# An attention loop on TensorE: scores, weighing and projection ahead of the subtraction of maxima and the turned scores

## The reference

```python
h = _L0_tok_ref(x, ...)                       # pairs of rows through a matrix, plus their mean, layer norm
h = h + _L0_attn_ref(_layernorm(h), ...)
h = h + _L0_ffn_ref(_layernorm(h), ...)       # shared FFN and 16 experts of 752 tokens each
...
latent_kv = (k + v) @ W_down_kv               # k = x @ W_k, v = x @ W_v
scores = einsum('bhqd,bhkd->bhqk', qh, k_rec) / sqrt(d) * exp(-0.01 * abs(t - t'))
out = einsum('bhqk,bhkd->bhqd', softmax(scores), v_rec) ; out @ W_o
```

## Time and profile before

| | before |
|---|---|
| time, median of 3 runs | 1873.16 us (1870.95 to 1875.5) |
| time of the profiled execution | 1870.4 us |
| its span | 1868.6 us |
| TensorE busy | 1689.0 us, 90% of the span |
| VectorE busy | 1224.8 us, 66% |
| ScalarE, GpSimd busy | 902.6 us, 950.2 us |
| mean granted clock of TensorE | 0.956 of 2.4 GHz |

### The profile page before, as it was taken

The page is one execution under the profiler, slowest core; times in us unless marked ns, Lnnn a source line. Parts: engine busy times, 40 slices in busy tenths (PEclk is TensorE's granted clock), DMA queues, the critical chain, the costliest instruction groups (busy, mean ns, idle before and its releaser), DMA issues.

```text
span 1868.6 us, 46715 instructions
## 1 busy us (share of the span) xinstructions
PE 1689.0 (90%) x15566; PEld 1232.2 (66%) x15566; DVE 1224.8 (66%) x3739; ACT 902.6 (48%) x1965; POOL 950.2 (51%) x945
## 2 busy tenths in 40 slices
PE   6874899999999999579999669999999999999997
PEld 5873566666666665357777537777777777777775
DVE  3883788888888888384778655555555555555551
ACT  4442566666666665244233634444444444444442
POOL 3771244444444443272224054666666666666665
PEclk9995999999999999789999779999999999999999
DMA  5522455555555555242010232333333334333322
GB/s 189 176 94 50 106 121 126 134 123 133 132 127 128 129 136 116 50 133 51 26 34 26 96 123 86 102 101 97 93 93 100 98 100 101 101 101 99 101 34 28
DMA packets 220234, 186.52 MB, mean 100 GB/s; under 512 B 165625, under 2 KB 200953, under 8 KB 214009
## 3 DMA queue, kind: packets, MB, share of 16 engines
q1 hardware_dynamic: 193272, 141.11, 28.2%
q0 software_dynamic: 26880, 44.36, 11.5%
HBM read 134.49 MB, written 50.44 MB: 99 GB/s over the span
## 4 chain that ended last, share of the span: by engine, by line
PE 70%; DVE 12%; issue 8%; POOL 4%; SPq 2%; ACT 2%; DMA 2%; DVEq 1%; POOLq 0%; ACTq 0%
PE psum L1678 26%; PE psum L1695 13%; PE psum L1542 6%; PE psum L1560 4%; DVE arena L1086 4%; DVE psum L1094 3%; PE psum L1441 3%; PE psum L1498 2%; PE psum L1395 2%; PE psum L1409 2%; PE psum L1463 2%; PE psum L1420 2%; POOL hidden L570 2%; POOL arena L575 1%; PE psum L1508 1%
## 5 line engine op out<-in xcount | busy, mean ns | idle before, releaser
L1678 PE MATMUL psum<-arena,hidden 128*128 128x376 f16 x3072 | 493.1, 323 | 0.9 <-DVE arena L1320 0.9
L634 POOL TENSOR_TENSOR arena<-arena 128x376 f16<-128x376 f32 x320 | 317.4, 994 | 343.9 <-ACT arena L727 342.5
L1678 PEld LDWEIGHTS psum<-arena,hidden 128*128 128x128 f16 x3072 | 301.0, 98 | 188.9 <-issue 1.6
L727 ACT ACTIVATE arena<-arena 128x376 f16<-128x376 f32 (+5 forms) x610 | 287.3, 474 | 54.0 <-DVE arena L1250 43.1
L1086 DVE CUSTOM_DVE_ANT_0 arena<-psum,constants 128x188 f32<-128x188 f32 x768 | 228.0, 345 | 106.8 <-PE psum L1395 105.4
L727 ACT ACTIVATE arena<-psum 128x188 f32<-128x188 f32 (+7 forms) x457 | 168.1, 398 | 257.6 <-PE psum L1658 74.9
L926 ACT ACTIVATE arena<-psum 128x376 f32<-128x376 f32 x256 | 123.7, 483 | 342.2 <-PE psum L1678 342.2
L1330 DVE SCALAR_TENSOR_TENSOR arena<-psum,arena 128x376 f32<-128x376 f32 x256 | 140.8, 550 | 189.3 <-ACT arena L926 187.8
L1695 PE MATMUL psum<-hidden,arena 128*128 128x256 f16 (+1 forms) x2304 | 256.6, 273 | 0.0
L1695 PEld LDWEIGHTS psum<-hidden,arena 128*128 128x128 f16 (+1 forms) x2304 | 229.8, 103 | 21.8
L776 ACT ACTIVATE arena<-psum 128x564 f32<-128x564 f32 x256 | 164.0, 641 | 98.6 <-PE psum L1409 97.0
(11 more groups left out here) (156 smaller groups left out, 2644.2 us busy)
## 6 DMA issues: line engine op xcount, KB each, us to landing
arena<-q_halves SPq DMA_DIRECT2D x384, 47.0 KB, 2.4
arena<-k_halves SPq DMA_DIRECT2D x384, 47.0 KB, 2.3
arena<-e_g SPq DMA_DIRECT2D x16, 1024.0 KB, 5.1
arena<-e_u SPq DMA_DIRECT2D x16, 1024.0 KB, 5.2
arena<-e_d SPq DMA_DIRECT2D x16, 1024.0 KB
arena<-x_t SPq DMA_DIRECT2D x32, 376.0 KB, 3.5
weighed<-arena POOLq DMA_DIRECT2D x32, 376.0 KB, 3.9
q_halves<-arena SPq DMA_DIRECT2D x32, 188.0 KB, 3.1
```

The costliest lines, as they stand in the source:

```text
L634: nc.gpsimd.tensor_tensor(dst, f, hi, ALU.subtract).then_inc(ready, 1)
L727: return nc.scalar.activation(dst, src, ACT.Copy, scale=scale)
L1678: last = mm(bank[2 * (s % 2) + i][:, 0:CHUNK], w_, a, start=n == 0, stop=n == 5)
```

## The change

In each step of the attention loop TensorE issues S, W, J, T, U where it issued S, T, U, W, J. The parts themselves, their waits, and the orders of the other engines are as before.

```diff
@@ -1515,10 +1515,10 @@
             def batch(b, par):
                 for j in range(HP):
                     scores(b, par, j)
+                    weigh(b, par, j)
+                    job(b, par, j)
                     take_max(b, par, j)
                     turned_scores(b, par, j)
-                    weigh(b, par, j)
-                    job(b, par, j)
 
             batches(pe, batch)
             meet(pe)
```

## The result

| | before | after |
|---|---|---|
| time, median | 1874.33 us (1870.95 to 1879.8, 4 runs) | 1978.4 us (1974.67 to 1979.41, 4 runs) |
| time of the profiled execution | 1870.4 us | 1974.67 us |
| VectorE busy share of 400 to 500 us | 87% | 76% |
| mean granted clock | 0.956 | 0.959 |

The changed kernel takes 1.0553 times as long (95% interval 1.0533 to 1.0574). The forecast was 1968, the range 1918 to 1992.

A forecast was written before the change was run, and what follows sets the result against it. TensorE and VectorE were taken to wait for each other in turn, 18.04 us a batch. New waits of 5.17 us less 1.85 won, over 27 batches, plus about 5 at the ends, gave 1873 + 95 = 1968 us; range 1918 to 1992.

The forecast's parts named there:

- Wait 1: TensorE's J4 waits for VectorE's add_out, which comes behind D3 and so U3; loss 1.48 us a batch.
- Wait 2: TensorE's J2 waits for ScalarE's copy of XF, behind E1 and so T1; loss 0.75 us a batch.
- Wait 3: TensorE's W7 waits for the turned maxima, VectorE's low_max behind D6; loss 1.01 us a batch.
- Wait 4: TensorE's S7 waits for VectorE's R6, reckoned from U5 by way of D5; loss 0.59 us a batch.
- Wait 5: TensorE's W1, W3, W5 wait for ScalarE's E of the step before; loss 0.28 us each, 0.84 a batch.
- Wait 6: TensorE's J1 waits for VectorE's normalized rows, made behind D0; loss 0.50 us, between 0.19 and 0.81.
- the gain: Six TensorE waits ahead of T4, T5, T7, W7, S0 and T0 go: up to 1.85 us a batch.
- the ends: The five batches at each end have only parts of the waits and gain: together about 5 us.
- A: Releasers of W and J come earlier too, so the new waits are not there: 1819 us; chance 0.07.
- B: Only VectorE's releases bind, ScalarE answers faster: 1.7 us a batch, +51, 1924 us; chance 0.12.
- D: Gain and loss cancel within about 0.2%, or the engine does not do what is written: 1873 us; chance 0.02.
- C: TensorE's clock falls to 0.50 once in each of 27 batches, near 2.9 us each: 2046 us; chance 0.05.

The follow-up runs named there:

- decay_last: Changed kernel with VectorE's small work (except inverse sums and moments' aggregation) ahead of D in each step and ScalarE's XF copy ahead of E1: 1934.61 us, ratio 1.0335.
- xf_early: Changed kernel with ScalarE's copy of XF ahead of E in its step 1 instead of behind it: 1965.97 us, ratio 1.0469.
- divisors_first: step5_only with SP's four reads of the inverse sums ahead of its write of the query halves: 1910.11 us, ratio 1.0185.
- inverse_in_4: divisors_first with VectorE's aggregation of the row moments in step 7 and its inverse sums in step 4: 1924.39 us, ratio 1.0258.
- weigh_late: J alone moved ahead (S, J, T, U, W in a step), with J5 also waiting for ScalarE's copy (os_ready): 1932.84 us, ratio 1.0309.
- step5_only: Kernel before with J ahead of T and U in step 5 alone, J5 also waiting on os_ready: 1867.47 us, ratio 0.9965.

## Why the prediction was right

The mechanism was the one that was put down, and each wait was where it was said. Below is what each cost in the batch shown: how long behind its forerunner a group starts, less how long that is where nothing holds it. Beside it stands the price in the prediction.

- Wait 1, J4 on add_out: 418.95 - 417.21 - 0.26 = 1.48; foretold 1.48. D3 starts 0.52 behind U3 where 0.60 was taken, and J4 0.12 behind add_out where 0.05 was taken; the two cancel, so that the match to 0.01 is luck.
- Wait 2, J2 on XF: 413.31 - 412.15 - 0.31 = 0.85; foretold 0.75.
- Wait 3, W7 on low_max: 405.49 - 404.06 - 0.41 = 1.02; foretold 1.01.
- Wait 4, S7 on R6: S7 loads 0.76 behind U6 (403.30), where 0.25 is usual, that is 0.51; foretold 0.59.
- Wait 5, W on E: 0.46, 0.38 and 0.38 in steps 1, 3 and 5, 1.22 together; foretold 0.84. This is the term that was mis-sized most. E2 starts 0.55 behind T2 and W3 0.11 behind E2's end, where 0.50 and 0.05 were taken.
- Wait 6, J1 on the normalized rows: 411.34 - 409.98 - 0.91 = 0.45 in this batch and 0.63 in the next; foretold 0.50, from 0.19 to 0.81. The mean of the 26 is 0.53, and that it comes so near is luck again. The prediction took the middle between a fast pair and a slow one, 1.03 us, and the pair was slow in 25 of the 26 batches: 1.06 to 1.51 us there, and 1.31 in the mean of all. Against that W1 stood 0.46 where 0.28 was taken, and D0 started 0.52 behind U0 (408.87, 409.39) where 0.60 was taken.

What makes the pair slow can be read from the traces. Each of its two instructions lasts 0.40 us alone. One that starts while GpSimd's product of the division (L614) is at work ends 0.14 to 0.15 us behind the end of that product, whenever it started: in 13 of 26 batches of the kernel before, as at 415.12 of the earlier trace rows, and in 25 of 26 of the changed kernel, as here, where the product runs from 409.81 to 410.81. An instruction that had started before the product keeps its 0.40 us. In decay_last, where the pair comes earlier and meets no such product, it takes 0.73 in all 26. The Trainium skill, GPSIMD Engine Reference, section Specifications, says that GpSimd shares its SBUF interfaces with VectorE and contends with some of its instructions. These traces agree with that, and give the size.

The sum is 5.5 to 5.7 against 5.17, 5.57 in the mean of the 26, and the gain, 1.85, was there in full: in these batches T waits for D nowhere. The balance would be 3.7. The period rose by 3.46 us in the mean of 26 batches, by 3.57 over the undisturbed ones of before, for 3.32 foretold. So more was won than the 1.85: that sum leaves out two losses of the kernel before, J4's own 0.21 idle behind add_out (422.81 of the earlier trace rows) and 0.12 ahead of S5. With them the balance is 3.4, and the 0.2 that is left is not explained. Waits and gain were both taken too small, and the forecast came out as near as it did because the two errors cancel in part.

The measured rise is 9 us more than the 95 foretold. 26 x 3.46 makes 90 of the 104.3 us, and the 27th full batch would be another 3.5, so that about 4 of the 9 lie in the full batches. The rest, some 11 us, is at the ends, to which the prediction gave 5: from the first to the last load of J5 the stage grew by 99.6 (666.5 against 566.9), and 4.7 lie outside it. What they consist of is not known.

One sentence of wait 1 is wrong and changes nothing: between U3 and J4 stood S4, T4, U4 and also W3, which the new order puts ahead of U3. The intervals there are counted from U3's start, and they hold.

Of the rivals, A (1819) falls by the result and decay_last; B (1924) by the table, since ScalarE's releases bind, and by more than foretold, 2.07 us for 1.59; D by the result. C, the clock, falls too: 1.47 us of idleness in each batch leave it at 1.00 in the profiled execution, and the mean granted clock of the other three executions, 0.954 to 0.956, is within what the kernel before has (0.953 to 0.962). But it is nearer than that sounds. In the run xf_early, J4's idle time of 1.48 us was followed by a fall in one batch and by none in the others. In divisors_first there was one behind 2.67 idle us, and in inverse_in_4 none behind 2.44. In this order (columns of rows 1; a clock of 0.50 would be 1.2 GHz throughout):

```profile
644.00:647.60 3.60, 2.02 (x28) 1.02 (x25) 3.01 (x10) 2.46 (x7) 1.34 (x2) 1.00 0.78 200
647.60:651.60 4.00, 3.96 (x33) 3.27 (x37) 1.96 (x9) 1.76 (x5) 1.21 (x2) 0.57 0.66 129
...
396.40:400.60 4.20, 1.79 (x18) 1.38 (x18) 2.65 (x10) 1.94 (x5) 1.22 (x2) 1.00 0.66 131
400.60:404.60 4.00, 3.93 (x33) 1.68 (x33) 1.75 (x8) 1.05 (x2) 0.17 (x1) 0.57 0.53 109
404.60:408.60 4.00, 3.76 (x54) 2.68 (x46) 3.35 (x17) 3.02 (x7) 0.73 (x2) 1.00 0.34 77
...
464.20:468.20 4.00, 3.90 (x48) 2.46 (x49) 2.59 (x13) 2.07 (x6) 1.47 (x2) 1.00 0.61 133
```

So the length of the idle time just before does not decide it alone. The price of a fall can be read as well. The batch of xf_early with the fall took 21.98 us, for a mean of 21.1. In weigh_late, where the clock fell three times behind 1.89 to 2.05 idle us of J1, two of these batches took 21.31 and 21.21, where a quiet one takes 20.0. That is 0.9 to 1.3 us, and the prediction's C had taken 2.9.

One step of the prediction was true and still not the whole: that J2 waits for XF. It had a second releaser, GpSimd's low half, which in the changed kernel ended 0.69 us ahead of J2 (411.72 + 0.90, against 413.31), and which only xf_early brought out. For the forecast it made no difference; for every mend of the change it does.

## What to carry to other kernels

In a loop that several engines share, an instruction that moves up loses as cover the work that it overtakes, if that stood between it and what causes its release. It also loses what moves up past the cause: J4 overtook T4 and U4, and W3 now stands ahead of U3, so that of its distance from U3 only S4 is left. Before moving one, look for rows in which it already starts at once behind its releaser: here three groups did, and they paid 0.85 to 1.48 us each. Price a removed wait by what stands second, on the same instruction and on the next ones: taking 1.47 us away gave back 0.7 to 0.9, taking 1.02 away 0.2. And of a reordering that loses as a whole one member may gain, if nothing that it needs is late: J5 alone was worth 0.35% (0.23 to 0.47).

## What was not expected of the hardware

SP wrote the query halves to memory and had to wait until they had landed before it read them back. When that write was issued later, this wait came to 2.4 us a batch, up to 3.6, and TensorE's S5 came to wait too. The kernel was 43 us slower than step5_only, of which S5's 1.4 us a batch account for 38.

GpSimd's product held a VectorE instruction that started during it until 0.15 us after its own end, and left one alone that had started earlier. So VectorE's pair of 0.72 us took 1.06 to 1.51 in the changed kernel wherever the product had begun ahead of one of its two instructions.

The clock tolerated more than I had feared: eight idle times in each 21.6 us, the longest 1.47 us, with TensorE busy 78%, left it at 1.00. Still there was one fall behind 1.48 us in xf_early, three behind 1.89 to 2.05 us in weigh_late, and none behind 2.44 us in inverse_in_4.
